# Output layer of sixteen experts: 64-token tiles paired as halves of one tile, weights on two semaphores, tokens asked one step earlier

## What is computed

```python
capacity = _capacity(s, N_EXPERTS)            # 1.25 * 4096 / 16 = 320
gate_logits = tokens.astype(jnp.float32) @ gate_w.T
combine_weights, sec_mask = _top1_router(gate_logits, capacity)
dispatch = jnp.einsum('sec,sd->ecd', sec_mask.astype(tokens.dtype), tokens)
h = jax.nn.gelu(jnp.einsum('ecd,edf->ecf', dispatch, w1))      # w1: 16 x 128 x 512
expert_out = jnp.einsum('ecf,efd->ecd', h, w2)                 # w2: 16 x 512 x 128
out = jnp.einsum('sec,ecd->sd', combine_weights.astype(tokens.dtype), expert_out)
...
x = _layernorm(x + _L0_attn_ref(x, ...), axis=-1)
x = _layernorm(x + _L0_ffn_ref(x, L0_ffn_gate_w, L0_ffn_w1, L0_ffn_w2), axis=-1)
x = _layernorm(x + _L1_attn_ref(x, ...), axis=-1)
x = _layernorm(x + _L1_ffn_ref(x, ...), axis=-1)
```

## Time and profile before

| | |
|---|---|
| runs, us | 859.24, 860.22, 860.17 |
| median, us | 860.17 |
| the profiled execution, us | 861.25 |
| its span, first to last instruction, us | 859.5 |
| mean granted TensorE clock | 0.96 |
| TensorE, VectorE, ScalarE, GpSimd busy, us | 765.3, 532.3, 462.2, 311.3 |
| expert stage, first transposition to last matmul, us from the span's start | 245.1 to 341.6 |

### The profile page before, as it was taken

One profiled execution on the slowest core, in us unless ns is written; L12 is line 12 of the kernel. 1 busy time (PEld: TensorE's weight loads), 2 busy tenths in 40 slices (PEclk: granted clock), 3 DMA queues, 4 the chain that ended last, 5 costly groups with the idle time before them and its releaser, 6 DMA issues.

```text
span 859.5 us, 19417 instructions
## 1 busy us (share of the span) xinstructions
PE 765.3 (89%) x7228; PEld 429.9 (50%) x7228; DVE 532.3 (62%) x1409; ACT 462.2 (54%) x733; POOL 311.3 (36%) x470
## 2 busy tenths in 40 slices
PE   3699999999559998389999999998999999999992
PEld 2244444444237777135555556554665555566441
DVE  5579999997502111556568766557666666636556
ACT  2598889898412221146445545444454455455675
POOL 6034344433471000624344443334433433224505
PEclk9999999999769999589999999999999999999996
DMA  4334444443144552312344533355433444222003
GB/s 160 84 102 126 132 133 129 113 111 98 40 97 131 154 155 69 104 35 73 77 100 106 106 83 70 65 100 106 85 72 65 97 93 94 58 57 55 1 1 98
DMA packets 111737, 78.04 MB, mean 91 GB/s; under 512 B 12528, under 2 KB 103088, under 8 KB 111648
## 3 DMA queue, kind: packets, MB, share of 16 engines
q1 hardware_dynamic: 106256, 70.38, 34.0%
q0 software_dynamic: 3664, 5.70, 2.7%
q10 hardware_dynamic: 1728, 0.79, 0.4%
HBM read 37.86 MB, written 13.63 MB: 60 GB/s over the span
## 4 chain that ended last, share of the span: by engine, by line
PE 36%; SPq 9%; DVE 7%; DMA 3%; issue 3%; POOL 1%; ACT 1%; ACTq 0%; DVEq 0%; POOLq 0%
PE l_ps_c L1320 7%; PE l_ps_v L1347 7%; PE l_ps_v L1248 4%; SPq L115 4%; PE l_ps_d L1333 4%; SPq L113 4%; PE l_by_query L1269 2%; DMA q_ring<-l_max_rows 2%; DVE l_rden L1899 2%; PE l_by_query L1260 2%; PE l_by_key L1302 1%; DVE l_neg_max L1887 1%; PE l_by_key L1440 1%; PE l_ps_m L1440 1%; PE l_by_query L1430 1%
## 5 line engine op out<-in xcount | busy, mean ns | idle before, releaser
L1887 DVE TENSOR_REDUCE l_neg_max<-l_by_query 128x6 bf16<-128x768 f32 x125 | 119.5, 956 | 120.0 <-PE l_by_query L1273 119.9
L2167 POOL TENSOR_SCALAR_AFFINE_SELECT l_probs<-l_probs 128x512 f32<-128x512 f32 x128 | 85.2, 666 | 204.8 <-ACT l_probs L1593 204.4
L1593 ACT ACTIVATE l_probs<-l_by_key 128x768 f32<-128x768 f32 x128 | 103.7, 810 | 68.1 <-PE l_by_key L1305 63.5
L508 ACT ACTIVATE l_probs<-l_ps_s,minus_bound 128x1024 f32<-128x1024 f32 x128 | 135.4, 1118 | 0.3 <-PE l_ps_s L386 0.2
L1320 PE MATMUL l_ps_c<-l_probs,l_values 128*64 128x256 f32 (+1 forms) x1024 | 112.2, 340 | 0.0
L1320 PEld LDWEIGHTS l_ps_c<-l_probs,l_values 128*64 128x64 f32 x1024 | 62.3, 136 | 39.1 <-issue 19.4
L401 PE MATMUL l_ps_o<-l_probs,l_vpad 128*32 128x256 f32 x1024 | 79.3, 392 | 0.2
L1614 ACT ACTIVATE l_values<-l_ps_v 128x512 f32<-128x512 f32 x64 | 38.2, 597 | 73.4 <-PE l_ps_v L1248 73.4
L1248 PE MATMUL l_ps_v<-w_v,l_xT 128*128 128x512 f32 x128 | 73.8, 659 | 0.4 <-ACT l_values L1614 0.4
L2175 POOL DMA_INDIRECT l_eg<-eout_d,fetch x32 | 33.8, 1058 | 90.1 <-POOLq L896 82.5
L1347 PE MATMUL l_ps_v<-w_o,l_ctx 128*128 128x128 f32 x512 | 66.4, 283 | 0.0
(11 more groups left out here) (280 smaller groups left out, 1419.7 us busy)
## 6 DMA issues: line engine op xcount, KB each, us to landing
l_rrep<-rden_d SPq DMA_DIRECT2D x32, 512.0 KB
q_ring<-l_parts SPq DMA_DIRECT2D x192, 64.0 KB
k_ring<-l_parts SPq DMA_DIRECT2D x180, 64.0 KB
w_both<-in_L_ffn_w_dram SPq DMA_DIRECT2D x32, 256.0 KB, 3.1
disp_d<-zeros SPq DMA_DIRECT2D x8, 320.0 KB, 5.3
l_xin<-in_L_attn_x_dram SPq DMA_DIRECT2D x16, 128.0 KB, 3.5
l_xr<-in_L_attn_x_dram SPq DMA_DIRECT2D x16, 128.0 KB, 3.6
x_d<-l_x SPq DMA_DIRECT2D x16, 128.0 KB, 3.8
```

The source lines that it names most:

```text
L508: act.activation(probs[c % RING][:, :], ps_s[c % 2][:, :], ACT.Exp, bias=k["minus_bound"][:, :], scale=SCALE).then_inc(probs_sb, 1)
L1593: act.activation(probs[c % P_RING][:, :, 0:N + P], by_key[:, :, 0:N + P], ACT.Exp, scale=SCALE).then_inc(p_sb, 1)
L1887: dve.tensor_reduce(neg_max[:, :, half, :, h].rearrange("p a u -> p u a"), query_scores(b, c)[:, :, 0:3 * P].rearrange("p u (a q) -> p u a ...
L2167: pool.affine_select(out=corners, in_=corners, compare_op=ALU.is_ge, fill=0.0, base=0, pattern=[[0, 4], [1, P]], channel_multiplier=-1).th ...
```

## The change

In the output layer the full tiles of each expert are computed as before. The small tile of an even expert is no longer computed with it but with the next, odd expert's: for each of the four hidden chunks one matmul of the even expert into output partitions 0 to 63 and one of the odd expert into 64 to 127, of the same columns of `ps_y[1]`. The even expert's activations and second weights have to live until then: there are four `hT` buffers, two of them in the space of `x3`, which this stage doesn't use otherwise. VectorE copies the 128 partitions of both small tiles at once into `y_rest`, and SP stores its halves in two transfers after the odd expert. The semaphore `w_in` becomes `w1_in` and `w2_in`. SP asks for the first weights of expert e+4 at the step's beginning, once expert e's hidden layer is done; then for the tokens of expert e+4 (before: e+3), once expert e+2's are transposed; then stores; and at odd experts, once the output layer is done, for the second weights of two experts. TensorE waits for the first weights ahead of the hidden layer and for the second ahead of the output layer. `copies` counts VectorE's output copies: 1, 3, 4, 6 after the four experts of a turn.

```diff
--- before.py
+++ after.py
@@ -324,9 +324,9 @@
             def expert_weights(n):
                 e, second = divmod(n, 2)
                 if second:
-                    sp.dma_start(k["w2"][e], w2[e].rearrange("(f p) c -> p f c", p=P)).then_inc(k["w_in"][e], 16)
+                    sp.dma_start(k["w2"][e], w2[e].rearrange("(f p) c -> p f c", p=P)).then_inc(k["w2_in"][e], 16)
                 else:
-                    sp.dma_start(k["w1"][e], w1[e]).then_inc(k["w_in"][e], 16)
+                    sp.dma_start(k["w1"][e], w1[e]).then_inc(k["w1_in"][e], 16)
 
             sp.dma_start(xin[0][:, :, :], rows(x, 0)).then_inc(x_in[0], 16)
             sp.dma_start(w_qkv[:, :], Wqkv).then_inc(w_qkv_in, 16)
@@ -893,6 +893,8 @@
 
     TILES = [(t, min(P, CAP - t)) for t in range(0, CAP, P)]
     FULL = CAP // P
+    REST = CAP % P
+    assert 2 * REST == P
     with ExitStack() as ctx:
         sb = lambda name, shape, dt: ctx.enter_context(nc.sbuf_tensor("ex_" + name, shape, dt))
         pb = lambda name, shape, dt: ctx.enter_context(nc.psum_tensor("ex_" + name, shape, dt))
@@ -900,16 +902,20 @@
         two = range(2)
         xe = [sb(f"xe{i}", [P, len(TILES), C], FP32) for i in two]
         xeT = [sb(f"xeT{i}", [P, CAP], FP32) for i in two]
+        later = k["x3"][:, :, :].rearrange("p a b -> p (a b)")
         hT = [sb(f"hT{i}", [P, FC, CAP], FP32) for i in two]
-        ye = [sb(f"ye{i}", [P, len(TILES), C], FP32) for i in two]
+        hT += [later[:, i * FC * CAP:(i + 1) * FC * CAP].rearrange("p (f n) -> p f n", n=CAP) for i in two]
+        ye = [sb(f"ye{i}", [P, FULL, C], FP32) for i in two]
+        y_rest = sb("y_rest", [P, C], FP32)
         ps_x = pb("ps_x", [P, 512], FP32)
         ps_h = [pb(f"ps_h{i}", [P, FC // 2, 512], FP32) for i in two]
         ps_y = [pb(f"ps_y{i}", [P, 512], FP32) for i in two]
         xe_in, ye_out = [sem(f"xe_in{i}") for i in two], [sem(f"ye_out{i}") for i in two]
+        rest_out = sem("rest_out")
         cleared, later_in, rows_set = (sem(n) for n in ("cleared", "later_in", "rows_set"))
         xeT_ps, xeT_sb, h_ps, h_sb, y_ps, y_sb = (sem(n) for n in ("xeT_ps", "xeT_sb", "h_ps", "h_sb", "y_ps", "y_sb"))
         block = ctx.enter_context(nc.Block())
-        w1_sb, w2_sb, w_in = k["w1"], k["w2"], k["w_in"]
+        w1_sb, w2_sb, w1_in, w2_in = k["w1"], k["w2"], k["w1_in"], k["w2_in"]
         W = len(w1_sb)
         w1, w2 = a["L0_ffn_w1"], a["L0_ffn_w2"]
         real = lambda e: not isinstance(e, int) or 0 <= e < E
@@ -925,29 +931,43 @@
                 yield r[FULL * P:CAP, :], sbuf[0:CAP % P, FULL, :]
 
         LOADS = 16 * len(list(tiles(disp_d, 0, xe[0])))
-        ye_parts = [(slice(0, P), slice(0, FULL))] + ([(slice(0, CAP % P), slice(FULL, FULL + 1))] if CAP % P else [])
+
+        def copies(he, q):
+
+            return he * 6 + (1, 3, 4, 6)[q]
+
+        def rows(dram, e, first, n):
+            return dram[e * CAP + first:e * CAP + first + n, :] if isinstance(e, int) else dram[bass.ds(e * CAP + first, n), :]
 
         @block.sync
         def _(sp):
             def step(e, he, q):
                 p = q % 2
-                if real(e + 3):
-                    wait_apart(sp, k, (xeT_ps, e + 2))
-                    for dram, sbuf in tiles(disp_d, e + 3, xe[1 - p]):
-                        sp.dma_start(sbuf, dram).then_inc(xe_in[1 - p], 16)
+                if real(e) and real(e + W):
+                    wait_apart(sp, k, (h_ps, (e + 1) * 2))
+                    sp.dma_start(w1_sb[q][:, :], expert(w1, e + W)).then_inc(w1_in[q], 16)
+                if real(e + 4):
+                    wait_apart(sp, k, (xeT_ps, e + 3))
+                    for dram, sbuf in tiles(disp_d, e + 4, xe[p]):
+                        sp.dma_start(sbuf, dram).then_inc(xe_in[p], 16)
                 if real(e):
-                    wait_apart(sp, k, (y_sb, (e + 1) * len(ye_parts)))
-                    for dram, sbuf in tiles(eout_d, e, ye[p]):
-                        sp.dma_start(dram, sbuf).then_inc(ye_out[p], 16)
-                if real(e) and real(e + W):
+                    wait_apart(sp, k, (y_sb, copies(he, q)))
+                    full = rows(eout_d, e, 0, FULL * P).rearrange("(t p) c -> p t c", p=P)
+                    sp.dma_start(full, ye[p][:, :, :]).then_inc(ye_out[p], 16)
+                    if p == 1:
+                        sp.dma_start(rows(eout_d, e - 1, FULL * P, REST), y_rest[0:REST, :]).then_inc(rest_out, 16)
+                        sp.dma_start(rows(eout_d, e, FULL * P, REST), y_rest[REST:P, :]).then_inc(rest_out, 16)
+                if real(e) and real(e + W) and p == 1:
 
                     wait_apart(sp, k, (y_ps, e + 1))
-                    sp.dma_start(w1_sb[q][:, :], expert(w1, e + W)).then_inc(w_in[q], 16)
-                    sp.dma_start(w2_sb[q][:, :, :], expert(w2, e + W).rearrange("(f p) c -> p f c", p=P)).then_inc(w_in[q], 16)
-
-            pipelined(sp, step, 3, 0, E, W)
+                    for d in (1, 0):
+                        sp.dma_start(w2_sb[q - d][:, :, :], expert(w2, e + W - d).rearrange("(f p) c -> p f c", p=P))\
+                          .then_inc(w2_in[q - d], 16)
+
+            pipelined(sp, step, 4, 0, E, W)
             for i in two:
-                sp.wait_ge(ye_out[i], LOADS * E // 2)
+                sp.wait_ge(ye_out[i], 16 * E // 2)
+            sp.wait_ge(rest_out, 32 * E // 2)
 
         @block.tensor
         def _(pe):
@@ -956,7 +976,7 @@
                 half = lambda d: (he * W + q + d) // 2 if isinstance(he, int) else he * (W // 2) + (q + d) // 2
                 if real(e + 1):
                     qn = (q + 1) % W
-                    pe.wait_ge(w_in[qn], ((he + (q + 1) // W) + 1) * 32)
+                    pe.wait_ge(w1_in[qn], ((he + (q + 1) // W) + 1) * 16)
                     pe.wait_ge(xeT_sb, e + 2)
                     for f in range(FC):
                         if f % 2 == 0:
@@ -972,12 +992,21 @@
                         last = pe.transpose(ps_x[:, t:t + n], xe[p][0:n, t // P, :], k["ident"][0:n, 0:n])
                     last.then_inc(xeT_ps, 1)
                 if real(e):
+                    pe.wait_ge(w2_in[q], (he + 1) * 16)
                     pe.wait_ge(h_sb, (e + 1) * 2)
-                    at_least(pe, y_sb, (e - 1) * len(ye_parts))
-                    for t, n in TILES:
+                    if q >= 2:
+                        pe.wait_ge(y_sb, copies(he, q - 2))
+                    elif not isinstance(e, int) or e >= 2:
+                        pe.wait_ge(y_sb, copies(he - 1, q + 2))
+                    for t in range(FULL):
                         for f in range(FC):
-                            last = pe.matmul(ps_y[p][0:n, t // P * C:(t // P + 1) * C], hT[p][:, f, t:t + n],
+                            last = pe.matmul(ps_y[p][:, t * C:(t + 1) * C], hT[q][:, f, t * P:(t + 1) * P],
                                              w2_sb[q][:, f, :], start=f == 0, stop=f == FC - 1)
+                    if p == 1:
+                        for f in range(FC):
+                            for d, half in ((1, slice(0, REST)), (0, slice(REST, P))):
+                                last = pe.matmul(ps_y[1][half, FULL * C:(FULL + 1) * C], hT[q - d][:, f, FULL * P:CAP],
+                                                 w2_sb[q - d][:, f, :], start=f == 0, stop=f == FC - 1)
                     last.then_inc(y_ps, 1)
 
             pipelined(pe, step, 2, 0, E, W, first=2)
@@ -985,12 +1014,11 @@
         @block.scalar
         def _(act):
             def step(e, he, q):
-                o = 1 - q % 2
                 if real(e + 1):
                     for i in two:
                         act.wait_ge(h_ps, (e + 1) * 2 + i + 1)
                         at_least(act, y_ps, e)
-                        act.activation(hT[o][:, 2 * i:2 * i + 2, :], ps_h[i][:, :, 0:CAP], ACT.Gelu_apprx_tanh).then_inc(h_sb, 1)
+                        act.activation(hT[(q + 1) % W][:, 2 * i:2 * i + 2, :], ps_h[i][:, :, 0:CAP], ACT.Gelu_apprx_tanh).then_inc(h_sb, 1)
 
             pipelined(act, step, 2, 0, E, W, first=1)
 
@@ -1013,10 +1041,11 @@
                     dve.tensor_copy(xeT[p][:, :], ps_x[:, 0:CAP]).then_inc(xeT_sb, 1)
                 if real(e):
                     dve.wait_ge(y_ps, e + 1)
-                    at_least(dve, ye_out[p], LOADS * half(0))
-                    for r, c in ye_parts:
-                        dve.tensor_copy(ye[p][r, c, :], ps_y[p][r, c.start * C:c.stop * C].rearrange("p (t c) -> p t c", c=C))\
-                           .then_inc(y_sb, 1)
+                    at_least(dve, ye_out[p], 16 * half(0))
+                    dve.tensor_copy(ye[p][:, :, :], ps_y[p][:, 0:FULL * C].rearrange("p (t c) -> p t c", c=C)).then_inc(y_sb, 1)
+                    if p == 1:
+                        at_least(dve, rest_out, 32 * half(0))
+                        dve.tensor_copy(y_rest[:, :], ps_y[1][:, FULL * C:(FULL + 1) * C]).then_inc(y_sb, 1)
 
```

(3 more changed lines are left out.)

## The result

| | before | after |
|---|---|---|
| runs, us | 857.95, 859.24, 860.17, 860.22 | 846.81, 849.71, 850.39, 854.21 |
| median, us | 859.70 | 850.05 |
| profiled execution, us | 861.25 | 850.39 |
| its span, us | 859.5 | 848.6 |

The ratio of the runs is 0.9877, with a 95% interval of 0.9848 to 0.9906: 1.2% faster. The forecast was 851.0 in a range of 849.0 to 854.0. The fourth run of before was added with the result.

The account below looks back on a forecast made before the run. TensorE was taken as the bound, busy all of the expert stage's steady part. Removed work -9.7, added work and loads 0, tail +0.5 sum to -9.2 us: from the median 860.17 to 851.0, range 849.0 to 854.0.

Parts of the forecast that it names:

- The removed block and shape changes: Even expert's output layer: 8 narrow instructions, both shape changes and an exposed weight load go, 1.21 us a pair, 9.7 in all.
- The added eight instructions at 0: Odd expert's narrow block: 8 more instructions overlap the 8 that stay in two column halves, adding 0 us.
- The nearest row: Second layer's context product: 8 instructions in two column halves took 0.80 us where one after another would need 1.28.
- The loads' order at 0: SP's queue in the expert stage: separate weight loads and the new order cost 0, hidden by TensorE; token slack 4.4 us.
- the cover's price: Token loads on SP: with the ask left at its old place, about 0.1 us a pair would come back.
- The tail: After the stage's last matmul: the third store is on the path, +0.5 us.
- Start and rest: Stage start as before, later work the same but 9 us earlier; clock's place up to 1.5 us either way, in the range.
- the two covers: Expert stage: tokens asked earlier and second weights waited for apart, cost 0; without one, each microsecond of wait costs a microsecond.
- no overlap: Rival, narrow block: the 16 instructions run in turn, 7.0 us come back, 858.0; chance 0.05.
- exposed loads: Rival, narrow block: weight loads show between the halves, 2.8 us in all (853.8) or 5.6 (856.6); chance 0.08.
- SP as the bound: Rival, SP's queue: twelve issues a pair become the bound, up to 889 us, chance 0.04; milder form about 860, 0.03.

Follow-up runs that it names:

- late_tokens: The changed kernel with the tokens of expert e+3 asked for at the old place, three steps ahead; 865.78 us, ratio 0.9994 to the kernel before.
- both_weights: The changed kernel with TensorE waiting for both weights of an expert ahead of its hidden layer; 869.18 us, ratio 1.0048 to the kernel before.

## Why the prediction was right

*The removed block and shape changes*: 1.21 us a pair were forecast, 9.7 in all. Measured: 1.20 a pair, 9.65 in the stage. Both parts stand in the slices: 0.11 and 0.27 at the seam.

*The added eight instructions at 0*: right. The block kept its 1.02 us, in twos 0.11 apart. The nearest row, the second layer's context product, decided it against the Trainium skill, "TensorE: Matmul & The Clock Gate" (Part 3, The mechanism), by whose rule that a weight load overlaps running matmuls only when its row group differs the loads of column halves would show: here too the two loads began under running matmuls of the same rows. The same section of the Trainium skill also lets a load run ahead into the background weight buffer, which the prediction left out; the rows don't tell by which way these loads ran. What the prediction left unsaid is that this depends on the written order: wholly in turn costs 0.49 a pair.

*The loads' order at 0*: right in sum and wrong in a step. SP's pair was estimated with the last token issue beginning 5.3 us after the odd expert's end; it begins at 277.62 + 1.10 - 0.54, 6.0 after 272.15, for the pauses of the loop's turn and the three stores' longer course. That still left 3.7 us. The step that failed is the cover's price, "about 0.1 us a pair" with the ask left at its old place. It was worked out from SP's order of before, with the short expert taking 1.1 of a slack of 1.0. But the pairing puts three stores and two second weights ahead of that ask, where two stores and an expert's two weights stood. The second token load, asked for some 4.1 us after the expert's end by the prediction's working, was asked for 4.9 to 5.9 us after the odd expert's end in five pairs of late_tokens (5.9 in the one shown: 268.25 to 274.2). It is 0.9 us of idle TensorE a pair, 5.5 in all, and 8.5 with exposed loads and half clock. A queue's slack has to be counted in the new order, and I did so for the new place of the ask only.

*The tail*: +0.5 forecast, +0.67 measured, as a store's issue took 0.59 there.

*Start and rest*: forecast as unchanged. They moved by -1.1 and -0.8 in the pair of profiles, and by several us in others, in code that is the same. The range gave 1.5 us for this and the runs of after spread over 7.4; that the median fell 1 us from the forecast was luck to that degree.

*The rivals*: no overlap would have shown starts evenly 0.11 apart, exposed loads twos 0.16 apart, SP as the bound idle TensorE; the profile after shows none. TensorE did wait for loads as soon as one of the two covers was taken away, 5.5 us for tokens or 9.9 us for second weights.

## What to carry to other kernels

In this kernel, float32 with 128 moving columns, a tile that fills half of TensorE's columns costs as much as a full one, and two of them in different halves cost as one, if the program writes them in alternation. Going over to another tile shape and back cost 0.33 us in the output layer and 0.29 in the transpositions, so group by shape. Before a busy engine's stage is shortened, count the transfer queue again in its new order: a reordering that gives nothing alone (1.0001) can be what the gain rests on (0.9994 without it). And where a kernel's time moves by several us between chips and runs, compare the changed stage inside the profiles, where 0.05 us could be told.

## What the runs showed that I had not expected

- By the starts, TensorE takes up instructions for a free column half ahead of earlier written ones for the busy half, within limits: with groups of eight the other half joined at the fifth, with groups of four at the first, and the block lost 0.05 us only.
- One wait of 1.63 us in an otherwise busy stage was followed by a stretch at half clock (278.30 to 281.60), which cost another 1.6 us. both_weights had a wait of 2.1 us without such a stretch in its stage.
- With twelve matmuls in the gap the clock stayed up over it and fell at 344.7 us, into a stretch in which TensorE was busy three quarters of the time.
- The stage's first transposition, behind code whose work no edit changed, started between 243.8 and 252.6 us, and within 3.7, 1.7 and 2.6 us of each other on the three chips.
